# Picking the two best experts per token: whole-chunk comparisons and maxima in place of MAX8 and FIND_INDEX8

## The reference

```python
logits = xf @ gate_w + gate_b                 # 8192 tokens x 8 experts
probs = softmax(logits)
top2_vals, top2_idx = top_k(probs, 2)
cw = zeros((N, 8)).at[arange(N)[:, None], top2_idx].add(top2_vals)
for e in range(8):                            # dense: every expert runs on every token
    h = gelu(xf @ W1[e] + b1[e]); y = h @ W2[e] + b2[e]
    acc = acc + cw[:, e] * y
```

## Time and profile before

| | |
|---|---|
| median of 3 runs | 214.54 us (211.86 to 216.39) |
| the profiled execution's own time | 214.92 us |
| its span | 213.1 us |
| PE busy | 169.5 us (80%) |
| DVE busy | 140.8 us (66%), 456 instructions |
| ACT busy | 117.1 us (55%) |
| POOL busy | 124.4 us (58%) |
| granted TensorE clock, mean | 0.908 |

### The profile page before, as it was taken

How to read it: one execution, slowest core, us unless ns; L and a number is a source line. 1 busy time by engine, 2 the same in 40 slices (tenths; PEclk the granted TensorE clock), 3 DMA queues, 4 the chain that set the end, 5 groups by cost and what they waited for, 6 DMA issues and landing times.

```text
span 213.1 us, 4043 instructions
## 1 busy us (share of the span) xinstructions
PE 169.5 (80%) x1211; PEld 87.0 (41%) x1211; DVE 140.8 (66%) x456; ACT 117.1 (55%) x153; POOL 124.4 (58%) x118
## 2 busy tenths in 40 slices
PE   3987203990079974979979999999999999999990
PEld 3874201360036762435434434344344344445530
DVE  0899999304975779966936848758459458344452
ACT  2368800134103784744697676676666766667750
POOL 7697106620096523514676777677757857858583
PEclk9999755697559996699999999999999999999998
DMA  5960000000000000494771893875946938939901
GB/s 163 316 92 0 3 2 0 0 3 0 0 0 0 3 0 0 109 210 95 195 183 22 218 218 107 208 156 148 200 105 156 210 87 193 210 107 215 219 1 49
DMA packets 16178, 22.39 MB, mean 105 GB/s; under 512 B 2202, under 2 KB 7970, under 8 KB 16162
## 3 DMA queue, kind: packets, MB, share of 16 engines
q1 hardware_dynamic: 16002, 22.04, 44.1%
q10 hardware_dynamic: 160, 0.15, 0.3%
HBM read 19.82 MB, written 2.36 MB: 104 GB/s over the span
## 4 chain that ended last, share of the span: by engine, by line
PE 53%; DVE 16%; DMA 9%; issue 8%; ACT 5%; POOL 4%; SPq 1%; POOLq 1%; DVEq 1%; ACTq 0%
PE ps L1057 20%; PE ps L1073 18%; PE ps L985 8%; DMA gbc<-gate_rows 5%; PE ps L942 4%; DVE xn L630 3%; DMA gate_rows<-gateT 2%; POOL x L403 2%; DMA x_sb<-in_x 2%; DVE ssum L618 2%; POOL qpad L355 1%; DVE gbc L693 1%; ACT work L422 1%; PE ps L1012 1%; ACT hl L493 1%
## 5 line engine op out<-in xcount | busy, mean ns | idle before, releaser
L403 POOL TENSOR_TENSOR x<-x,y_sb 128x512 f32 (+1 forms) x63 | 80.2, 1273 | 39.7 <-DVE y_sb L846 34.9
L546 ACT ACTIVATE work<-ps,bias_sb,w_back 128x1024 f32<-128x1024 f32 x64 | 76.9, 1203 | 37.3 <-PE ps L1057 37.1
L846 DVE SCALAR_TENSOR_TENSOR y_sb<-ps,bias_sb,gbc 128x512 f32<-128x512 f32 x64 | 47.5, 749 | 41.2 <-PE ps L1073 32.8
L1073 PE MATMUL ps<-work,w_sb 128*64 128x512 f32 x256 | 66.0, 594 | 0.5 <-DVE y_sb L846 0.4
L1057 PE MATMUL ps<-xT,w_hi 128*64 128x512 f16 x256 | 39.9, 389 | 1.1 <-ACT work L546 1.1
L1057 PE MATMUL ps<-xT,w_lo 128*64 128x512 f16 x256 | 39.3, 385 | 0.0
L985 PE MATMUL ps<-qpad,cw_bd 128*128 128x512 bf16 x72 | 21.4, 456 | 21.9 <-POOL qpad L355 21.9
L1057 PEld LDWEIGHTS ps<-xT,w_hi 128*64 128x64 f16 x256 | 14.2, 111 | 32.7 <-issue 30.2
L1073 PEld LDWEIGHTS ps<-work,w_sb 128*64 128x64 f32 x256 | 18.4, 137 | 13.2 <-ACT work L546 3.0
L985 PEld LDWEIGHTS ps<-qpad,cw_bd 128*128 128x128 bf16 x72 | 7.7, 110 | 33.1 <-issue 15.9
L1057 PEld LDWEIGHTS ps<-xT,w_lo 128*64 128x64 f16 x256 | 15.5, 112 | 12.9 <-issue 1.0
(11 more groups left out here) (106 smaller groups left out, 177.3 us busy)
## 6 DMA issues: line engine op xcount, KB each, us to landing
gbc<-gate_rows SPq DMA_DIRECT2D x16, 768.0 KB, 9.7
gbc<-gate_rows SPq DMA_DIRECT2D x16, 256.0 KB, 3.8
x_sb<-in_x SPq DMA_DIRECT2D x8, 256.0 KB, 5.4
out<-x SPq DMA_DIRECT2D x8, 256.0 KB, 10.2
w_raw<-in_W SPq DMA_DIRECT2D x2, 256.0 KB, 6.6
w_sb<-in_W SPq DMA_DIRECT2D x1, 256.0 KB
gate_rows<-gateT SPq DMA_DIRECT2D x8, 32.0 KB, 3.6
cw<-in_conv_w ACTq DMA_DIRECT2D x2, 72.0 KB, 3.8
```

Of the source, the lines that this page charges most:

```text
L403: pool.tensor_tensor(x2[:, ds(c * W, W)], x2[:, ds(c * W, W)], y_sb[:, u % H_RING, :], ALU.add).then_inc(added, 1)
L546: act.activation(h_sb[:, u % H_RING, :], bank(H + 2 * (u % 2), 2 * W), ACT.Gelu, bias=b1_sb[:, u:u + 1], scale=w_back[:, u:u + 1]).then_in ...
L846: dve.scalar_tensor_tensor(y_sb[:, u % H_RING, :], bank(Y + u % 2), b2_sb[:, u:u + 1], gbc[:, slot, u, :], ALU.add, ALU.mult).then_inc(wei ...
L1073: last = pe.matmul(ps[r * CH:(r + 1) * CH, (Y + u % 2) * W:(Y + u % 2 + 1) * W], w2_sb[:, u, :], h_sb[:, u % H_RING, r * W:(r + 1) * W], s ...
```

## The change

The eight values per group are no longer sorted. For a whole chunk at once (128 partitions, 8 groups, 8 experts), with logits from which the group's maximum has been taken (`shifted`, so the best is 0): compare with 0 and multiply by a falling iota (8 for expert 0, 1 for expert 7), take the maximum per group, and the place where the product equals it is the first expert (the lowest index where two are equal). That place is pushed to a very low value, the maximum of the rest is taken, and the same is done again for the second. 27 DVE instructions of a chunk (the copy, 8 MAX8, 8 MATCH_VALUE_LOAD, 8 FIND_INDEX8, 2 comparisons) become 9: one scalar_tensor_tensor and a maximum in unit 0, a comparison, a scalar_tensor_tensor and a maximum in unit 1, a comparison, a product and a maximum in unit 2, a comparison in unit 3. The shifted logits get a tensor of their own, and the exponentials are read from it.

```diff
-            link(pool.iota(iota_i[:, :, :], pattern=[[0, GROUPS], [1, EXPERTS]], base=0, channel_multiplier=0))
+            link(pool.iota(iota_i[:, :, :], pattern=[[0, GROUPS], [-1, EXPERTS]], base=EXPERTS, channel_multiplier=0))
...
-                act.activation(ex[:, first:last, :, :], ex[:, first:last, :, :], ACT.Exp).then_inc(exp_ready, 1)
+                act.activation(ex[:, first:last, :, :], shifted[:, first:last, :, :], ACT.Exp).then_inc(exp_ready, 1)
...
-            def route_copy(c):
-                mark(dve.tensor_copy(lcur[:, :, :], logit[:, ds(c, 1), :, :].rearrange("p z g e -> p (z g) e")))
-
-            def route_max(groups):
-                settled(stand=True)
-                for g in groups:
-                    last = dve.max(top[:, g, :], lcur[:, g, :])
-                mark(last)
-
-            def route_index(groups):
-                settled(stand=True)
-                for g in groups:
-                    last = dve.max_index(topi[:, g, :], top[:, g, :], lcur[:, g, :])
-                mark(last)
...
+            def route_first(c):
+                dve.wait_ge(z_ready, 1 + (c // 2 if isinstance(c, int) and c < EARLY else 2))
+                settled()
+                link(dve.scalar_tensor_tensor(rank1[:, :, :], shifted_of(c), 0.0, iota_e[:, :, :],
+                                              ALU.is_ge, ALU.mult))
+                mark(dve.tensor_reduce(peak[:, 0, :], rank1[:, :, :], AX.X, ALU.max))
+
+            def route_rest(c):
+                settled()
+                link(dve.tensor_tensor(sel1[:, :, :], rank1[:, :, :], wide_g(peak[:, 0, :]), ALU.is_equal))
+                link(dve.scalar_tensor_tensor(rest[:, :, :], sel1[:, :, :], -3e38, shifted_of(c),
+                                              ALU.mult, ALU.add))
+                mark(dve.tensor_reduce(peak[:, 1, :], rest[:, :, :], AX.X, ALU.max))
+
+            def route_second():
+                settled()
+                link(dve.tensor_tensor(rank2[:, :, :], rest[:, :, :], wide_g(peak[:, 1, :]), ALU.is_equal))
+                link(dve.tensor_tensor(rank2[:, :, :], rank2[:, :, :], iota_e[:, :, :], ALU.mult))
+                mark(dve.tensor_reduce(peak[:, 2, :], rank2[:, :, :], AX.X, ALU.max))
+
             def route_select():
                 settled()
-                dve.tensor_tensor(sel1[:, :, :], iota_e[:, :, :], wide_e(topi[:, :, 0:1]), ALU.is_equal)
-                mark(dve.tensor_tensor(sel2[:, :, :], iota_e[:, :, :], wide_e(topi[:, :, 1:2]), ALU.is_equal))
+                mark(dve.tensor_tensor(sel2[:, :, :], rank2[:, :, :], wide_g(peak[:, 2, :]), ALU.is_equal))
...
                     if route and u == 0:
-                        route_copy(c + 2)
                         route_sum(c + 2)
+                        route_first(c + 2)
                     if route and u == 1:
-                        route_max(range(GROUPS))
+                        route_rest(c + 2)
                     if route and u == 2:
-                        route_index(range(GROUPS))
+                        route_second()
...
-            PER = 6
+            PER = 11
```

More of the change, by code:

```diff
@@ L86, in program @@
         ex = sb("ex", [128, NCH, GROUPS, EXPERTS])
-        lcur = sb("lcur", [128, GROUPS, EXPERTS])
-        top = sb("top", [128, GROUPS, 8])
-        topi = sb("topi", [128, GROUPS, 8], u32)
+        shifted = sb("shifted", [128, NCH, GROUPS, EXPERTS])
+        rank1 = sb("rank1", [128, GROUPS, EXPERTS])
+        rank2 = sb("rank2", [128, GROUPS, EXPERTS])
+        rest = sb("rest", [128, GROUPS, EXPERTS])
+        peak = sb("peak", [128, 3, GROUPS])
         esum = sb("esum", [128, GROUPS])
@@ L790, in shifted_logits @@
                 link(dve.tensor_reduce(m, l, AX.X, ALU.max))
-                dve.tensor_tensor(ex[:, first:last, :, :].rearrange("p z g e -> p (z g) e"), l,
+                dve.tensor_tensor(shifted[:, first:last, :, :].rearrange("p z g e -> p (z g) e"), l,
                                   m.unsqueeze(2).to_broadcast([128, n, EXPERTS]), ALU.subtract).then_inc(z_ready, 1)
-            def route_copy(c):
-                mark(dve.tensor_copy(lcur[:, :, :], logit[:, ds(c, 1), :, :].rearrange("p z g e -> p (z g) e")))
-            def route_max(groups):
-                settled(stand=True)
-                for g in groups:
-                    last = dve.max(top[:, g, :], lcur[:, g, :])
-                mark(last)
-            def route_index(groups):
-                settled(stand=True)
-                for g in groups:
-                    last = dve.max_index(topi[:, g, :], top[:, g, :], lcur[:, g, :])
-                mark(last)
             wide_e = lambda a: a.to_broadcast([128, GROUPS, EXPERTS])
@@ L818, in route_sum, with shifted_of @@
                 dve.tensor_reduce(esum[:, :], ex_of(c), AX.X, ALU.add)
+            def shifted_of(c):
+                return shifted[:, ds(c, 1), :, :].rearrange("p z g e -> p (z g) e")
+            wide_g = lambda a: a.unsqueeze(2).to_broadcast([128, GROUPS, EXPERTS])
+            def route_first(c):
[15 more added lines that the diff above has]
+                mark(dve.tensor_reduce(peak[:, 2, :], rank2[:, :, :], AX.X, ALU.max))
             def route_select():
                 settled()
-                dve.tensor_tensor(sel1[:, :, :], iota_e[:, :, :], wide_e(topi[:, :, 0:1]), ALU.is_equal)
-                mark(dve.tensor_tensor(sel2[:, :, :], iota_e[:, :, :], wide_e(topi[:, :, 1:2]), ALU.is_equal))
+                mark(dve.tensor_tensor(sel2[:, :, :], rank2[:, :, :], wide_g(peak[:, 2, :]), ALU.is_equal))
             def route_gates(c):
@@ L886, in _ @@
             shifted_logits(0)
-            settled()
-            route_copy(0)
+            route_first(0)
             invert(LN2_PARTS, 2, std2, rstd2)
-            route_max(range(GROUPS))
+            route_rest(0)
             normalise(4, LN2_PARTS, rstd2, xn2_ready)
-            route_index(range(GROUPS))
+            route_second()
             high_half(4)
@@ L902, in _ @@
             normalise(7, LN2_PARTS, rstd2, xn2_ready)
-            settled()
-            route_copy(1)
+            route_first(1)
             high_half(7)
             take_xT(4)
-            route_max(range(GROUPS))
+            route_rest(1)
             take_xT(5)
-            route_index(range(GROUPS))
+            route_second()
             route_sum(1)
```

## The result

Over 20 runs each the kernel after has a median of 215.24 us and the kernel before 214.78 us; the medians differ by 0.46 us. The ratio of the two kernels is 1.0082, 95% interval 1.0044 to 1.0119, that is 1.8 us more, within 0.9 to 2.6; it leaves out as slow every execution over 1.5% above the fastest of its kernel, 10 of before and 4 of after, and so sets after against the faster half of before. The kernel before scatters more (211.59 to 221.37 us; 15 of the 20 executions of after lie between 214.32 and 215.73). The profiled execution took 214.46 us with a span of 212.7 us.

A forecast was written before the change was run, and what follows sets the result against it. PE's own matmuls were taken as the bound, with routing on the path ahead of the expert stages; 0.1 + 0.45 + 0.6 + 1.2 = 2.35 us on 214.92 gave 217.2 us, range 213.4 to 220.4.

The forecast's parts named there:

- (c): Whole kernel: holds happen but all stay in the slack and the two starts cancel, 214.9 us; chance 0.21.
- Bound and holds: Expert stages: PE's matmuls bound; POOL additions hold two-SBUF-tensor DVE operations until 2.27 us after the weigh's start.
- DVE's busy time: Sign in the profile after: DVE's busy time hardly falls.
- PE's wait for weigh at the second product: Sign at line 1073: PE's wait for weigh grows from 0.4 to about 2 us.
- Slack of a weigh: Expert stages: a weigh may be 1.39 us late at no cost; overruns cost 0.6 us over chunks 1 to 3.
- Chunks 4 and 5: Weigh of unit 2 already late by broadcast gates; another 0.71 us exceeds the slack, 0.6 us each, 1.2 us.
- The start: Routing of chunks 0 and 1 ahead of the expert stages: +0.1 us and +0.45 us.
- The hold of route_rest: Chunk 1, ahead of the stages: the comparison of route_rest, issued at 89.1, is held for 1.1 us.
- Sum: Whole kernel: all terms add 2.35 us, giving 217.2 us.
- (a): Unit 0's scalar_tensor_tensor is held too, 0.7 us more in 5 chunks, about 220.4; chance 0.22 with other cases over 218.8.
- (b): DVE's queue priced by instruction count, no holds; routing of chunks 0 and 1 ends earlier, 213.4 us; chance 0.10.

The follow-up runs named there:

- e4: Kernel after, with one tensor operand of each two-tensor routing operation in the expert stages moved to PSUM; median 217.36 us of 6 runs.
- e9: Kernel after with fp16 gates and POOL's additions cut to half their columns, so half the expert output is left out; 213.69 us in one run.
- e10: Kernel after with fp16 gates and, in the expert stages, only the first selection in PSUM; 211.68 us in one run.
- e7: Kernel after with fp16 gates and one operand of each two-tensor routing operation of the stages in PSUM; 212.87 us, ratio 0.9965.
- e8: Kernel after (fp32 gates) with, in the expert stages, only the first selection in PSUM; 216.26 us.
- second profile of before: The kernel before, unchanged, profiled once more; 215.62 us.
- e5: Kernel before with the gates stored, sent and broadcast as fp16, half the bytes; 212.63 us, ratio 0.9965.
- e12: Kernel after with fp16 gates and one more reduction of the exponentials ahead of route_first in the expert stages; 214.43 us.
- e6: Kernel after with the gates stored, sent and broadcast as fp16; 214.68 us, ratio 1.0037.
- e2: New routing only inside the expert stages (chunks 2 to 7), chunks 0 and 1 routed as in the kernel before; ratio 1.0115.
- e3: New routing only for chunks 0 and 1, ahead of the expert stages; the stages route as in the kernel before; ratio 1.0132.

## Why the prediction was right, and where it was off

It forecast a loss within 2% and got one: 1.2% forecast, 0.8% measured (0.4 to 1.2) by the ratio and 0.2% by the medians, 215.24 us inside the range. The mechanism that it gave is the one that the runs show. The number was less good: 215.24 lies below the 216 to 218.8 that the forecast itself had, and next to the 214.9 of rival (c), whose mechanism is wrong.

- **Bound and holds.** Right: two holds at 1.32 us in units 1 and 2, none in unit 0, second products delayed behind the weighs of units 3 and 5, chunks of 14.27 to 14.53 us where 14.3 to 15.3 was forecast. e4 and e9 show that it is POOL's whole operation and the two SBUF tensors that make the hold; e10 shows the slack. Two of the signs that it named came otherwise. DVE's busy time was to fall a little and rose by 15.2 us, of which the 12 holds of 1.1 us each are some 13 us (e7, without holds in the stages, has 139.4 us of DVE in all). PE's wait for weigh at the second product was to grow from 0.4 to 2 us in the list, where it reads 0.2; the delay is there, but in the chain. Nor had all that was removed one tensor: the two comparisons of a chunk that went (lines 822 and 823 of before) had two.
- **Slack of a weigh.** Right: 1.39 us. Mis-sized was the unit with the hold. In chunks 2 to 5 the weigh after unit 1 came 2.53 us on and not 2.43, because in DVE's loop it started 0.25 us after the reduction (129.50, the reduction at 129.25); in chunk 1, outside the loop, that step took 0.14. The weigh of unit 3 was then 2.53 + 2.44 - 3.44 = 1.53 us late, 0.14 over the slack, and the weigh of unit 5 added the rest. I also took 0.2 us a chunk in place of 0.3, as if a chunk after a delayed one might miss it; none did. Measured against the 14.12 us of an undisturbed chunk: 0.15, 0.39 and 0.41 in chunks 1 to 3, 0.95 us in all against the 0.6 that I took.
- **Chunks 4 and 5.** The step that failed. I took the lateness of the gates (1.2 and 1.7 us in the earlier trace rows) as given and put the hold on top, 1.2 us for both. The profile of after had no late gates: these chunks took 14.53 and 14.52 us against 14.22 and 14.73 before, +0.1 in all, and the last two chunks became 0.7 us faster, for which the prediction had no term. e8 shows that the combination that I priced exists (15.2 to 16.0 us), only not in this execution of after.
- **The start.** +0.55 forecast, 14.77 against 14.38 and 14.49 measured: +0.3 to 0.4. The hold of route_rest was 1.07 us as worked out.
- **Sum.** 0.4 + 0.95 + 0.1 - 0.7 = 0.75 us by these terms, 0.71 by the table, where 2.35 was forecast; against the second profile of before after is 0.3 us shorter. Without late gates (e5 to e7) it is 2.0 us, close to the 2.35, but partly by luck: the two holds in chunks 4 and 5 cost 0.8 there and not 1.2, those in chunks 1 to 3 0.95 and not 0.6. That the measured time lies in the range also owes something to its width of 7 us.
- **Rivals.** (a), slower by a hold in unit 0, did not happen, since the margin was larger (e12); what such a hold would cost was not measured. (Its price has a slip: 0.7 us in each of 5 chunks is 3.5 us, not 3.2.) (b), a gain by the count of instructions, fell with the start: 18 instructions fewer a chunk, and the start is longer. By "VectorE: DVE Perf Modes", "Rules for kernel authors", of the Trainium skill the count of operations is what to minimise; no stage here gains by it. (c) is refuted by C in e6 against e5, 72.36 and 70.62 us.

What is different where the gates are in time is the small transfer ahead of the broadcasts. The DMA queue of SP in after and then in before, chunk 5:

```profile
154.99 0.58 SPq L269 DMA_DIRECT2D gate_rows<-gateT  x1
157.39 3.01 SPq L278 DMA_DIRECT2D gbc<-gate_rows  x4
160.89 0.41 SPq L284 DMA_DIRECT2D out<-x  x1
```

```profile
154.83 0.58 SPq L267 DMA_DIRECT2D gate_rows<-gateT  x1
159.58 3.01 SPq L276 DMA_DIRECT2D gbc<-gate_rows  x4
```

The broadcasts go out 2.4 us after the 32 KB in after and 4.75 us in before. In the list of DMA issues these 32 KB take 2.2 us in the median in after, 3.6 and 4.5 in the two profiles of before, 3.3 to 3.9 in e2, e3, e4 and e8, and 1.8 as fp16 (16 KB). It fits that with chunks 0.4 us longer the broadcasts and the store of the chunk before are over when the next 32 KB start, but this is argued; e2 has the same longer chunks and waited 4.0 us for gates, so longer chunks alone don't settle it. Of the seven profiles with fp32 gates that of after is the only one without a wait for them. What decides it in one execution stays open, and whether after mostly runs so does too.

## What to carry to other kernels

Price a DVE operation by what runs beside it, not by its elements: ask of each new one whether it has two SBUF tensors and where the neighbour's long GpSimd operation stands; fewer instructions made DVE busier here. One hold in the slack is free, two in a row are not, and a PSUM operand in a free bank takes them away. Before a gain on one engine is counted, look for the transfer that is only just in time: here it took the gain of e4, and how late it was decided how much of the loss by the change one profile or one median shows.

## What the runs showed of the hardware

- A DVE operation with two SBUF tensors issued in a GpSimd tensor_tensor waits for its end: 1.33 us beside 1.28, 0.79 beside 0.72. With one tensor in PSUM it takes 0.23 us in the same place. In after each such operation of units 1 and 2 ended 0.08 us after the addition. This is the exclusive lock of the Trainium skill, "SBUF — State Buffer", "SBUF: two separate sides", and the traces agree with it: reductions, MAX8 and weigh were not held; the copy of the earlier trace rows, with one tensor, was.
- Operations of 64 elements a partition with a PSUM operand took 0.21 to 0.23 us, no longer than those in SBUF (0.21 to 0.23).
- A transfer of 32 KB took 2.2 us in the median in after and up to 5.25 us in before; 16 KB with half the traffic around it took 1.8 us.
